# A median found from a bracket with two ends, folded coefficients, and another order of the input, at the head of a conv-attention-MoE layer

## The chip, the cores and the metric

The kernel runs on one core of a Trainium2 chip. The metric is the device time of one execution in microseconds (us); the median of three runs is given. Engines are named as in the profile: PE is TensorE's matmuls and PEld its weight loads, DVE is VectorE, ACT is ScalarE, POOL is GpSimd, SP is SyncE, which issues most DMAs.

## The reference

The input x is 8 batches of 512 channels of 16 x 16. The layer normalises x by groups of 16 channels, gates each channel by its own statistics, and goes on with windowed attention (16 heads) and a mixture of 8 experts over 2048 tokens. The change touches the gate alone:

```
xf = x.reshape(b, c, h * w)                       # x: normalised by groups
mean, mx, std = mean(xf), max(xf), std(xf, ddof=1)     # over 256 places, per channel
u = stack([mean, mx, std], axis=-1)               # per batch 512 * 3 = 1536 numbers
med = median(u.reshape(b, -1), axis=-1)           # mean of the 768th and the 769th
u = (u - med) ** 3
z = einsum('bck,ck->bc', u, cfc_w) / sqrt(1 + eps) * bn_w + bn_b
return x * sigmoid(z)                             # and x + this goes on as tokens
```

## The kernel before

All 8 batches of x lie in SBUF as T, channels on partitions (4 blocks of 128). SyncE loads them in the order 0 to 7 (L427), one semaphore each, then the attention's weights.

Statistics. For batches 0 to 3 ScalarE makes the sums and, after a pass with the means, the sums of squares (L699 to L709); VectorE makes the maxima of all 8 batches and the statistics of batches 4 to 7 (L967 to L973). A matmul with a group matrix gives the group's mean, another its variance. ScalarE then splits two pieces of the weights, loads the table for the square root, and takes it (L719). VectorE computes u, 128 partitions by 8 batches x 12 numbers (4 blocks, 3 kinds), and three copies spread so that TensorE's transposes put each batch's 1536 numbers on 16 partitions.

Median. In 8 rounds, each of the 16 partitions of a batch tests a threshold; VectorE and ScalarE count half of the numbers each, and a matmul adds the 16 answers, so the interval narrows by 16 in each round (L1041 to L1061). `low` is then a lower bound within the last width. What follows is exact: `low` is brought from the 128 threshold partitions to 96 rows (one for each batch, block and kind, holding 128 channels, `uT`); the numbers at most `low` are counted and the least above it is found; count and least go by transposes to one partition, where the 768th number is chosen; that goes back to the 96 rows, the same count and least are made for it, and the 769th is chosen; half their sum goes to all partitions by a matmul. These are five exchanges between VectorE and TensorE (`med_in`, `med_out`).

Coefficients. VectorE cubes u - med, multiplies by the weights, adds the three kinds, scales by the norm's constant and weight, adds its bias; ScalarE takes the exponential; VectorE forms the sigmoid, multiplies by 1/deviation and gets the two coefficients for each batch and channel (L1119 to L1142).

Then `affine(0)` applies them to batch 0 (L1145), TensorE transposes it to tokens (L1619), ScalarE copies the tokens, VectorE and GpSimd normalise them, TensorE transposes again and begins the projections. `keep_busy(n)` is n matmuls of the identity whose result nobody reads (L1570); each is two passes in the trace. They stand where TensorE would else be idle: 10, then 8 ahead of the rounds, 9 behind the median, 16 behind the first transposes. The order on each engine is as written; there is no scheduler. What stands behind (attention, experts, adding the experts' results into the output by a chain of DMAs) is the same in both versions.

Of the kernel before, what the change touches and what calls it, by code (L numbers as in the profile page):

```python
# [17 lines left out]
B, C, S = 8, 512, 256  # L18
# [3 lines left out]
P = 128  # L22
CB = C // P
# [3 lines left out]
UK = 3  # L27
ACT_STATS = 4
UP = CB * UK
MED_N = C * UK  # L30
CNT = 17
# [77 lines left out]
def layer_kernel(nc, x, params, wqkvo, gate, ws, wgu, wd, out):  # L109
    ctx = ExitStack()  # L110
    with ctx:

        def sb(name, shape, dt=fp32, scope=ctx):
            return scope.enter_context(nc.sbuf_tensor(name, shape, dt))
# [55 lines left out]
        row = sb("row", [1, 8, B * UP], fp32, scope)  # L170
        g_avg = sb("g_avg", [P, P], fp32, scope)
        spread = sb("spread", [P, B * UP], fp32, scope)
        col = sb("col", [B * UP, 24], fp32, scope)
        sb("below_rden", [P, 8], fp32, scope)
# [47 lines left out]
        u = vf[:, 0:B * UP]  # L222
        uw = vf[:, B * UP:4 * B * UP].rearrange("p (k n) -> p k n", k=3)
        uT = vf[0:B * UP, 4 * B * UP:4 * B * UP + P]
        junk = vf[0:B * UP, 4 * B * UP + P:4 * B * UP + 4 * P].rearrange("p (k n) -> p k n", k=3)

        is_below = vf[:, 4 * B * UP + 4 * P:4 * B * UP + 4 * P + 1].bitcast(bf16)[:, 0:1]
        block_sum = vf[:, 4 * B * UP + 4 * P + 2:4 * B * UP + 4 * P + 2 + P // 2].bitcast(bf16)
        iota_i = qf[:, 512:512 + P].bitcast(i32)
        token_i = qf[:, 768:768 + 2 * NT].bitcast(i32)  # L230
        every_u = [front[:, 0:512], front[:, 512:1024], x2[:, 0:512]]
# [104 lines left out]
        z_ready, ez_ready = sem("z_ready"), sem("ez_ready")  # L336
# [68 lines left out]
        NCONSTS = 7  # L405
# [106 lines left out]
        def _(pool):  # L512
            pool.wait_ge(fills_done, NFILLS)
            for t, base, pattern, mult, fill, op in (
# [3 lines left out]
                (spread[:, :].rearrange("p (a c) -> p a c", c=UP), 0, [[-THRESHOLDS, B], [0, UP]], 1, 1.0,  # L518
                 ALU.not_equal),
# [3 lines left out]
            pool.wait_ge(consts_done, 4)  # L523
# [166 lines left out]
        def _(act):  # L690
# [4 lines left out]
            cols = [(b, k, CB * b + k) for b in range(ACT_STATS) for k in range(CB)]  # L695
            na = CB * ACT_STATS
            unread = [t[:, S * k:S * (k + 1)] for t in (front, x2T, x2) for k in range(CB)]
            unread += [probs[:, k, 0:S] for k in range(CB)]
            for b, k, c in cols:  # L699
                act.wait_ge(x_loaded[b], 16)  # L700
                ins = act.activation(unread[c], at(T, b)[:, k * S:(k + 1) * S], ACT.Copy,
                                     accum_out=small[:, 12, c:c + 1])
            ins.then_inc(act_sums, 1)
            act.wait_ge(act_sums, 1)
            act.activation(small[:, 13, 0:na], small[:, 12, 0:na], ACT.Copy, scale=-1.0 / S).then_inc(act_sums, 1)
            act.wait_ge(act_sums, 2)
            for b, k, c in cols:
                ins = act.activation(unread[c], at(T, b)[:, k * S:(k + 1) * S], ACT.Square,
                                     bias=small[:, 13, c:c + 1], accum_out=small[:, 5, c:c + 1])  # L709
            ins.then_inc(act_sums, 1)  # L710
# [19 lines left out]
            act.activation(small[:, 15, :], small[:, 14, :], ACT.Exp, scale=-1.0).then_inc(ez_ready, 1)  # L730

# [205 lines left out]
        def _(dve):  # L937
# [8 lines left out]
            fill(spread[:, :], 0.0)  # L946
# [3 lines left out]
            lo, bound, cnt = col[:, 0:1], col[:, 1:2], col[:, CNT:CNT + 3]  # L950
# [13 lines left out]
            n.n = 4  # L964


            for b in range(B):  # L967
# [23 lines left out]
            dve.wait_ge(act_sums, 2)  # L991
# [6 lines left out]
            dve.wait_ge(act_sums, 3)  # L998
# [19 lines left out]
            dve.wait_ge(root_ready, 1)  # L1018
            dve.wait_ge(dve_step, step_of(dve.reciprocal(inv2, root)))
# [5 lines left out]
            u3 = u.rearrange("p (n k) -> p n k", k=UK)  # L1025
# [10 lines left out]
            dve.tensor_tensor(u3[:, :, 0], K(7), r, ALU.mult)  # L1036
            dve.tensor_tensor(u3[:, :, 1], K(10), r, ALU.mult)
            dve.scalar_tensor_tensor(u3[:, :, 2], root2[:, n32:2 * n32], 0.5, r, ALU.mult, ALU.mult).then_inc(u_ready, 1)
# [3 lines left out]
            for i, width in enumerate(WIDTHS):  # L1042
# [8 lines left out]
                if i == 0:  # L1051
                    dve.wait_ge(uT_full, 1)
                    dve.wait_ge(dve_step, step_of(dve.tensor_copy(uT, PS[6][0:B * UP, 0:P])))
# [6 lines left out]
                else:  # L1060
                    ins.then_inc(med_in, 1)  # L1061

            def least(dst, bound):

                dve.wait_ge(dve_step, step_of(dve.tensor_scalar(junk[:, 0, :], uT, bound, BIG, ALU.is_le, ALU.mult)))
                dve.wait_ge(dve_step, step_of(dve.tensor_tensor(junk[:, 1, :], junk[:, 0, :], uT, ALU.add)))
                return dve.tensor_reduce(dst, junk[:, 1, :], AX.X, ALU.min)

            def of_batch(k):
                return row[0:1, k, :].rearrange("p (b n) -> p b n", b=B)  # L1070


            def by_batch(t):
                return t.rearrange("p (b n) -> p b n", b=B)

            dve.wait_ge(med_out, 1)
            dve.wait_ge(dve_step, step_of(dve.tensor_copy(lo, PS[4][0:B * UP, 384:385])))
            step_of(dve.tensor_scalar(junk[:, 2, :], uT, lo, 0.0, ALU.is_le, ALU.add, accum_out=cnt[:, 1:2]))
            step_of(least(cnt[:, 0:1], lo))
# [932 lines left out]
```

## Time and profile before

| | |
|---|---|
| median of 3 runs | 718.38 us (717.37 to 720.6) |
| profiled execution | 718.36 us |
| its span, first to last instruction | 716.6 us |
| busy: PE, PEld, DVE, ACT, POOL | 649.3, 553.2, 443.4, 335.8, 317.5 us |
| mean granted TensorE clock | 0.965 |

The span is counted from the first instruction. A row of a timeline tells when an instruction or a group of like ones started, how long it was busy, and in brackets how long its engine idled before it and what ended that. Granted clock is the share of 2.4 GHz that TensorE was given: 1.00 or 0.50.

### The profile page before, as it was taken

The page shows a single profiled execution, that of the slowest core. Times are in us where ns is not written, and L with a number is a line of the kernel's source. Part 1 is how long each engine was busy: PE and PEld are TensorE (multiplying, and loading weights), DVE is VectorE, ACT ScalarE, POOL GpSimd, SP SyncE. Part 2 cuts the span into 40 slices and gives each one's busy share as a digit, 9 for nine tenths or more (in the row PEclk, how much of TensorE's full clock was granted, in tenths as well). Part 3 has the DMA queues.
Part 4 walks back from the last instruction along what each step waited for, and adds up shares of the span by engine and source line. Part 5 has one row for each costly group of instructions (what it writes and reads, how often), then busy time and mean ns, then how long its engine had stood idle before and what let it go on. Part 6 is the DMA issues. An engine that isn't in the chain of part 4 may idle for free.

```text
span 716.6 us, 14422 instructions
## 1 busy us (share of the span) xinstructions
PE 649.3 (91%) x5030; PEld 553.2 (77%) x5031; DVE 443.4 (62%) x974; ACT 335.8 (47%) x616; POOL 317.5 (44%) x377
## 2 busy tenths in 40 slices
PE   1417989999999999999999999999899999999991
PEld 1407878888888888887789899999677877778771
DVE  7875454757575757573646995223676767667761
ACT  7641364646464646465523123434444454444540
POOL 1340343646464646462421115856345455454534
PEclk9758999999999999999999999999999999999996
DMA  9800000101010101020226323452865555556543
GB/s 307 340 0 1 1 2 1 60 1 59 0 59 0 59 0 59 1 90 1 90 76 240 116 91 113 130 176 70 299 115 96 112 98 107 105 100 111 99 70 44
DMA packets 24787, 62.62 MB, mean 87 GB/s; under 512 B 3056, under 2 KB 7920, under 8 KB 23216
## 3 DMA queue, kind: packets, MB, share of 16 engines
q1 hardware_dynamic: 14912, 41.69, 16.3%
q0 software_dynamic: 9168, 20.45, 15.7%
q8 instruction: 21, 0.34, 0.2%
q10 hardware_dynamic: 672, 0.03, 0.1%
q14 instruction: 14, 0.11, 0.0%
HBM read 39.09 MB, written 23.07 MB: 87 GB/s over the span
## 4 chain that ended last, share of the span: by engine, by line
PE 53%; DMA 27%; DVE 10%; issue 4%; POOL 3%; ACT 1%; DVEq 1%; SPq 0%; POOLq 0%; ACTq 0%
DMA out_tokens<-yo,dest 24%; PE PS L1566 21%; PE scores L1566 12%; PE scores L1858 5%; PE PS L1686 4%; PE scores L1670 3%; PE PS L1635 2%; PE PS L1693 1%; DMA out_tokens<-T 1%; DVE rden L1203 1%; DMA T<-in_x 1%; DVE front L1046 1%; POOL out_tokens L668 1%; PE PS L1624 1%; DVE front L1150 1%
## 5 line engine op out<-in xcount | busy, mean ns | idle before, releaser
L1566 PE MATMUL scores<-xb,sw_h 128*128 128x256 f32 x512 | 94.6, 285 | 0.0
L659 POOL DMA_INDIRECT out_tokens<-yo,dest x36 | 57.1, 1586 | 79.6 <-DMA out_tokens<-yo,dest 77.3
L1566 PEld LDWEIGHTS scores<-xb,sw_h 128*128 128x128 f32 x512 | 81.2, 192 | 2.2 <-ACT probs L757 0.4
L1566 PE MATMUL PS<-xt_h,w_h 128*128 128x256 f32 x256 | 74.5, 291 | 1.6 <-DVE xt_l L1188 1.6
L1566 PE MATMUL scores<-xb,sw_l 128*128 128x256 f32 x256 | 72.5, 283 | 0.0
L1566 PE MATMUL PS<-xt_l,w_h 128*128 128x256 f32 x256 | 72.4, 283 | 0.0
L1566 PE MATMUL PS<-xt_h,w_l 128*128 128x256 f32 x256 | 72.3, 283 | 0.0
L558 POOL TENSOR_SCALAR_AFFINE_SELECT probs<-probs 128x256 f32<-128x256 f32 x128 | 50.4, 418 | 45.6 <-ACT probs L761 45.4
L1566 PE MATMUL scores<-wgu_h,xgT_h 128*128 x156 | 65.0, 417 | 2.1 <-DVE xgT_l L1528 2.1
L1203 DVE RECIPROCAL rden<-PS 128x256 f32<-128x256 f32 x32 | 56.1, 1753 | 13.5 <-PE PS L1686 11.8
L577 POOL TENSOR_TENSOR hl<-hf,hh 128x256 fp32r<-128x256 f32 x32 | 28.5, 890 | 76.3 <-ACT hh L839 76.3
L1566 PE MATMUL scores<-wgu_h,xgT_l 128*128 x156 | 61.1, 391 | 0.0
L907 ACT ACTIVATE wdt_h<-wd_sb 128x512 fp32r x76 | 43.9, 624 | 36.4 <-PE scores L1566 36.4
L1566 PE MATMUL scores<-wgu_l,xgT_h 128*128 x156 | 60.9, 390 | 0.0
L757 ACT ACTIVATE probs<-scores 128x768 f32<-128x768 f32 x64 | 51.3, 802 | 11.2 <-PE scores L1670 11.1
L761 ACT ACTIVATE probs<-probs 128x768 f32<-128x768 f32 x64 | 54.1, 846 | 2.0
L1523 DVE TENSOR_TENSOR wdt_l<-wd_sb,wdt_h 128x512 fp32r<-128x512 f32 x76 | 49.1, 688 | 9.3 <-ACT wdt_h L907 7.6
L1566 PEld LDWEIGHTS PS<-xt_h,w_h 128*128 128x128 f32 x256 | 49.0, 191 | 4.8 <-issue 3.0
L571 POOL TENSOR_TENSOR att_l<-att,att_h 128x256 fp32r<-128x256 f32 x32 | 23.8, 744 | 63.8 <-ACT att_h L765 63.7
L1566 PEld LDWEIGHTS scores<-xb,sw_l 128*128 128x128 f32 x256 | 49.1, 192 | 0.0
L1566 PEld LDWEIGHTS PS<-xt_l,w_h 128*128 128x128 f32 x256 | 49.0, 192 | 0.0
L1566 PEld LDWEIGHTS PS<-xt_h,w_l 128*128 128x128 f32 x256 | 49.0, 192 | 0.0
(304 smaller groups left out, 1623.6 us busy)
## 6 DMA issues: line engine op xcount, KB each, us to landing
wgu_l<-in_wgu SPq DMA_DIRECT2D x8, 1024.0 KB, 7.7
T<-in_x SPq DMA_DIRECT2D x8, 512.0 KB, 7.9
w_in<-in_wqkvo SPq DMA_DIRECT2D x4, 1024.0 KB, 12.1
x_rows<-x SPq DMA_DIRECT2D x8, 512.0 KB, 2.8
x_cols<-x2T SPq DMA_DIRECT2D x8, 512.0 KB, 2.6
xc<-x_cols SPq DMA_DIRECT2D x8, 512.0 KB, 3.9
out_tokens<-T SPq DMA_DIRECT2D x8, 512.0 KB, 7.8
wd_sb<-in_wd SPq DMA_DIRECT2D x8, 512.0 KB, 6.9
```

The costliest lines, as they stand in the source:

```text
L558: ins = pool.affine_select(out=t, in_=t, compare_op=ALU.is_ge, fill=0.0, base=0, pattern=[[0, 2], [1, P]], channel_multiplier=-1)
L571: pool.tensor_tensor(att_l[:, c, :], att[:, :], att_h[:, c, :].bitcast(fp32), ALU.subtract).then_inc(att_l_done, 1)
L577: pool.tensor_tensor(hl[:, j, :], hf[:, j % 2, :], hh[:, j, :].bitcast(fp32), ALU.subtract).then_inc(hl_done, 1)
L659: pool.indirect_dma_start(out[:, :], bass.IndirectOffsetOnAxis(dest[:, t:t + 1], 0), yo[:, t % 3, :], None, compute_op=ALU.add).then_inc(y ...
L757: act.activation(probs[:, p % 4, :].rearrange("p (h q) -> p h q", h=2), scores[:, 2 * (p % 2):2 * (p % 2) + 2, 0:384], ACT.Tanh, scale=1.0 ...
L761: act.activation(probs[:, p % 4, :], probs[:, p % 4, :], ACT.Exp, scale=SOFTCAP).then_inc(exp_done, 1)
L907: act.activation(wdt_h[:, k * C:(k + 1) * C], w[:, k * C:(k + 1) * C], ACT.Copy).then_inc(wdt_h_done, 1)
L1203: dve.wait_ge(dve_step, step_of(dve.reciprocal(rden[:, :], od_bank[:, S:2 * S])))
L1523: dve.tensor_tensor(wdt_l[:, k * C:(k + 1) * C], w[:, k * C:(k + 1) * C], wdt_h[:, k * C:(k + 1) * C].bitcast(fp32), ALU.subtract).then_in ...
L1566: ins = pe.matmul(out, lhs(k, a), rhs(k, b), start=m == 0, stop=m == len(products) - 1)
L1686: ins = pe.matmul(od_bank[j * D:(j + 1) * D, off + tt * P:off + S], lhs(h, tt), pr[:, 0:S] if tt == 0 else pr[:, S:S + P], start=tt == 0, ...
L1858: ins = pe.matmul(dn_bank[tt], (hh, hl)[a][:, j, tt * P:(tt + 1) * P], shared_slice(c, 2, j, 0, C), start=j == 0 and m == 0, stop=j == CB ...
```

## The change

1. SyncE loads x in the order 0, 1, 4, 2, 5, 3, 6, 7, and VectorE takes the batches in that order. ScalarE makes sums and squares for batches 0 and 1, and then for 2 and 3.
2. Each batch's 12 numbers lie in 16 places of u (the others hold a large number), so that the transpose has 128 rows, 16 for a batch, like the thresholds: `low` needs no exchange. An upper end `high` is `low` plus the last width and a rounding allowance. VectorE finds in each row the least number from `low` up, the negative of the greatest up to `high`, the least above `high`, and the count up to `high`. One matmul brings the four to 8 partitions, one for each batch; there the upper of the two middle numbers is the greatest up to `high`, or the least above it if the count falls short, and so on; a matmul of ones with a diagonal brings half the sum to all partitions.
3. The norm's constant and weight are multiplied into the convolution's weights beforehand (`weights3`); 1 + exp(-z) is multiplied by the deviation before the reciprocal.
4. Of `affine(0)`'s four blocks ScalarE makes two, with an Identity activation with scale and bias from the coefficients.
5. `keep_busy(9)` becomes `keep_busy(8)`.

```diff
-            for b in range(B):
+            for b in ARRIVAL:
                 sp.dma_start(at(T, b).rearrange("p (k s) -> p k s", k=CB),
...
+            for first, group in enumerate(((0, 1), (2, 3))):
+                these = [(b, k, CB * b + k) for b in group for k in range(CB)]
...
+            act.wait_ge(coef_ready, 1)
+            for k in (2, 3):
+                ins = act.activation(front[:, k * S:(k + 1) * S], at(T, 0)[:, k * S:(k + 1) * S], ACT.Identity,
+                                     bias=coefB[:, k:k + 1], scale=coefA[:, k:k + 1])
+            ins.then_inc(y0_upper, 1)
...
+            step_of(dve.tensor_scalar(deviation, root2[:, 0:n32], 0.5, None, ALU.mult))
+            dve.wait_ge(prm_loaded, 16)
+            step_of(dve.scalar_tensor_tensor(
+                weights3.rearrange("p (c k) -> p c k", k=UK), prm[:, 0:UP].rearrange("p (c k) -> p c k", k=UK), bn_scale,
+                prm[:, UP:UP + CB].unsqueeze(2).to_broadcast([P, CB, UK]), ALU.mult, ALU.mult))
...
+            size_step = step_of(dve.scalar_tensor_tensor(low_size, low, -1.0, low, ALU.mult, ALU.max))
+            from_low = step_of(dve.tensor_scalar(least_of[:, 0, :], uT, low, BIG, ALU.is_lt, ALU.mult))
+            dve.wait_ge(dve_step, size_step)
+            dve.wait_ge(dve_step, step_of(dve.tensor_scalar(low_size, low_size, 3.0 / 2 ** 23, WIDTHS[-1], ALU.mult,
+                                                            ALU.add)))
+            high_step = step_of(dve.tensor_tensor(high, low_size, low, ALU.add))
+            step_of(dve.tensor_tensor(least_of[:, 0, :], least_of[:, 0, :], uT, ALU.add))
+            dve.wait_ge(dve_step, high_step)
+            counted = step_of(dve.tensor_scalar(least_of[:, 2, :], uT, high, 0.0, ALU.is_le, ALU.add,
+                                                accum_out=cols[:, 3:4]))
+            over_high = step_of(dve.tensor_scalar(least_of[:, 1, :], uT, high, BIG, ALU.is_gt, ALU.mult))
+            dve.wait_ge(dve_step, counted)
+            step_of(dve.scalar_tensor_tensor(least_of[:, 2, :], least_of[:, 2, :], BIG, uT, ALU.mult, ALU.add))
+            dve.wait_ge(dve_step, over_high)
+            dve.wait_ge(dve_step, step_of(dve.tensor_tensor(least_of[:, 1, :], least_of[:, 1, :], uT, ALU.subtract)))
+            dve.wait_ge(dve_step, step_of(dve.tensor_reduce(cols[:, 0:3], least_of, AX.X, ALU.min)))
+            dve.tensor_tensor(cols_of, cols.unsqueeze(2).to_broadcast([P, 4, UM]),
+                              own_slot.unsqueeze(1).to_broadcast([P, 4, UM]), ALU.mult).then_inc(med_in, 1)
             dve.wait_ge(med_out, 1)
...
+            dve.wait_ge(dve_step, step_of(dve.tensor_reduce(count, by_slot[:, 3, :], AX.X, ALU.add)))
+            step_of(dve.tensor_reduce(rows[:, 0:3], by_slot[:, 0:3, :], AX.X, ALU.min))
...
+            dve.tensor_scalar(diagonal, ident[0:B, 0:B], both, 0.5, ALU.mult, ALU.mult).then_inc(med_in, 1)
...
+            dve.wait_ge(dve_step, step_of(dve.scalar_tensor_tensor(K(0), K(15), 1.0, deviation, ALU.add, ALU.mult)))
+            dve.wait_ge(dve_step, step_of(dve.reciprocal(K(2), K(0))))
...
+                for k in range(2 if isinstance(b, int) and b == 0 else CB):
...
+            pe.matmul(PS[4][0:B, 384:384 + 4 * UM], own_batch, cols_of.rearrange("p k j -> p (k j)"), start=True,
+                      stop=True).then_inc(med_out, 1)
             pe.wait_ge(med_in, 2)
+            pe.matmul(PS[6][:, 0:B], ones[0:B, :], diagonal, start=True, stop=True).then_inc(med_out, 1)
...
+                if part == "lead":
+                    pe.wait_ge(y0_upper, 1)
...
-            keep_busy(9)
+            keep_busy(8)
```

How the instructions stand on the engines is shown at three places. Names are those of the program: qT, kT, v and x (for x2) also hold the small tables of this stage, T is the input. First VectorE over the batches of the input, before:

```order
L973 TENSOR_REDUCE qT<-T 128x4 x4
L972 BN_STATS qT<-T 128x6 x4
L973 TENSOR_REDUCE qT<-T 128x4
L972 BN_STATS qT<-T 128x6 x4
L973 TENSOR_REDUCE qT<-T 128x4
L972 BN_STATS qT<-T 128x6 x4
L973 TENSOR_REDUCE qT<-T 128x4
L972 BN_STATS qT<-T 128x6 x4
L973 TENSOR_REDUCE qT<-T 128x4
```

and in the change:

```order
L987 TENSOR_REDUCE qT<-T 128x4 x2
L986 BN_STATS qT<-T 128x6 x4
L987 TENSOR_REDUCE qT<-T 128x4 x2
L986 BN_STATS qT<-T 128x6 x4
L987 TENSOR_REDUCE qT<-T 128x4 x2
L986 BN_STATS qT<-T 128x6 x4
L987 TENSOR_REDUCE qT<-T 128x4
L986 BN_STATS qT<-T 128x6 x4
L987 TENSOR_REDUCE qT<-T 128x4
```

A maximum (TENSOR_REDUCE) alone is a batch of ScalarE's; a maximum behind four BN_STATS is one of VectorE's own. Before, the four lone ones stood first; now the second and third stand between VectorE's own.

Then TensorE from the last round of the search (L1595, L1593) to the first transposes of batch 0 (L1624, L1615), before:

```order
L1595 MATMUL PS<-v 128x1 x8
L1598 MATMUL PS<-med,spread 96x1
L1600 MATMUL PS<-ident,col 1x96
L1601 MATMUL PS<-ident,col 1x96
L1602 MATMUL PS<-ident,col 1x96
L1604 MATMUL PS<-ones,row 96x1
L1606 MATMUL PS<-ident,col 1x96
L1607 MATMUL PS<-ident,col 1x96
L1609 MATMUL PS<-row,ones 128x8
L1574 MATMUL scores<-ident 128x128 x9
L1624 MATMUL PS<-ident,front 128x128 x8
```

and in the change:

```order
L1593 MATMUL PS<-v 128x1 x8
L1595 MATMUL PS<-x,qT 8x64
L1598 MATMUL PS<-x,ones 128x8
L1572 MATMUL scores<-ident 128x128 x8
L1615 MATMUL PS<-ident,front 128x128 x8
```

Of eight small instructions in five exchanges two are left, and the filler behind them has one matmul less.

Last VectorE from the last update of the bound (L1055, L1082) up to what TensorE carries to the place of the choice; before, with the first instruction behind that (L1083):

```order
L1055 SCALAR_TENSOR_TENSOR med<-PS,med 128x1
L1077 COPY col<-PS 96x1
L1078 TENSOR_SCALAR v,col<-v,col 96x128
L1065 TENSOR_SCALAR v<-v,col 96x128
L1066 TENSOR_TENSOR v<-v 96x128
L1067 TENSOR_REDUCE col<-v 96x1
L1083 TENSOR_REDUCE row<-PS 1x8
```

and in the change, up to the product that TensorE takes (L1106):

```order
L1082 SCALAR_TENSOR_TENSOR med<-PS,med 128x1
L1090 SCALAR_TENSOR_TENSOR x<-med 128x1
L1091 TENSOR_SCALAR v<-v,med 128x128
L1093 TENSOR_SCALAR x<-x 128x1
L1095 TENSOR_TENSOR x<-x,med 128x1
L1096 TENSOR_TENSOR v<-v 128x128
L1098 TENSOR_SCALAR v,x<-v,x 128x128
L1100 TENSOR_SCALAR v<-v,x 128x128
L1102 SCALAR_TENSOR_TENSOR v<-v 128x128
L1104 TENSOR_TENSOR v<-v 128x128
L1105 TENSOR_REDUCE x<-v 128x3
L1106 TENSOR_TENSOR x<-x,qT 128x64
```

Before, a copy of the bound from TensorE stands at the head, and the same four instructions come again later for the second number. Now eleven instructions stand in one piece, over 128 rows and for both ends, and the copy is gone.

## Rows read from the trace of the kernel before

**Rows 1.** Page, chain that ended last, shares of the span by engine.
```profile
PE 53%; DMA 27%; DVE 10%; issue 4%; POOL 3%; ACT 1%; DVEq 1%; SPq 0%; POOLq 0%; ACTq 0%
```

**Rows 2.** Windows: stretch, length; busy PE, PEld, DVE, ACT, POOL; clock; DMA, GB/s.
```profile
46.55:55.28 8.73, 2.70 (x12) 1.69 (x12) 4.96 (x27) 1.15 (x1) 0.00 (x0) 0.50 0.00 0
...
54.65:59.20 4.55, 4.55 (x20) 4.41 (x20) 3.21 (x14) 0.23 (x1) 0.00 (x0) 0.50 0.01 4
59.40:60.09 0.69, 0.00 (x0) 0.00 (x0) 0.64 (x2) 0.00 (x0) 0.00 (x0) 1.00 0.00 0
```

**Rows 3.** Timeline of VectorE, statistics: start, duration, engine, line, operation, tiles, [idle before].
```profile
8.13 1.22 DVE L973 TENSOR_REDUCE qT<-T 128x4 f32<-128x1024 f32 x1 [0.42 <-DMA T<-in_x]
...
11.29 1.41 DVE L972 BATCH_NORM_STATS2 qT<-T 128x6 f32<-128x256 f32 x4 [0.28 <-DMA T<-in_x]
12.62 1.20 DVE L973 TENSOR_REDUCE qT<-T 128x4 f32<-128x1024 f32 x1
...
21.15 0.19 DVE L988 TENSOR_TENSOR kT<-qT 128x16 f32<-128x16 f32 x1
21.25 0.18 DVE L989 TENSOR_TENSOR kT<-qT 128x16 f32<-128x16 f32 x1
```

**Rows 4.** Timeline of ScalarE: sums, squares, table load, square root.
```profile
11.00 0.40 ACT L701 ACTIVATE probs<-T 128x256 f32<-128x256 f32 x1
...
12.28 0.49 ACT L708 ACTIVATE front<-T,kT 128x256 f32<-128x256 f32 x1
...
21.67 1.28 ACT L719 ACT_TABLE_LOAD   x1
24.48 0.26 ACT L719 ACTIVATE kT<-kT 128x64 f32<-128x64 f32 x1 [1.52 <-DVE kT L1012]
```

**Rows 5.** Timeline of VectorE: last bound update, median, its subtraction.
```profile
46.55 0.16 DVE L1055 SCALAR_TENSOR_TENSOR med<-PS,med 128x1 f32<-128x1 f32 x1 [0.28 <-PE PS L1595]
...
47.48 0.34 DVE L1078 TENSOR_SCALAR_CACHE_REDUCE v<-v,col 96x128 f32<-96x128 f32 x1
...
47.75 0.28 DVE L1065 TENSOR_SCALAR v<-v,col 96x128 f32<-96x128 f32 x1
48.06 0.29 DVE L1066 TENSOR_TENSOR v<-v 96x128 f32<-96x128 f32 x1
48.38 0.28 DVE L1067 TENSOR_REDUCE col<-v 96x1 f32<-96x128 f32 x1
49.46 0.25 DVE L1083 TENSOR_REDUCE row<-PS 1x8 f32<-1x96 f32 x1 [0.79 <-PE PS L1602]
...
55.28 0.26 DVE L1119 TENSOR_TENSOR v<-v,PS 128x96 f32<-128x96 f32 x1 [0.68 <-PE PS L1609]
```

**Rows 6.** Timeline of VectorE: norm's scale, product with the deviation, affine step.
```profile
56.73 0.19 DVE L1130 SCALAR_TENSOR_TENSOR kT<-kT,prm 128x32 f32<-128x32 f32 x1
...
58.04 0.19 DVE L1139 TENSOR_TENSOR kT<-kT 128x32 f32<-128x32 f32 x1
...
58.66 1.38 DVE L1150 TENSOR_SCALAR front<-T,coefA,coefB 128x256 f32<-128x256 f32 x4
```

**Rows 7.** Timeline of TensorE: fillers and transposes.
```profile
14.42 4.37 PE L1574 MATMUL scores<-ident 128*128 128x128 f32 x20 [14.42 <-DMA T<-in_x]
...
55.17 4.21 PE L1574 MATMUL scores<-ident 128*128 128x128 f32 x18
60.09 1.09 PE L1624 MATMUL PS<-ident,front 128*128 128x128 f32 x8 [0.71 <-DVE front L1150]
61.02 3.74 PE L1574 MATMUL scores<-ident 128*128 128x128 f32 x32
65.80 1.09 PE L1635 MATMUL PS<-ident,front 128*128 128x128 f32 x8 [1.04 <-DVE front L1173]
```

**Rows 8.** Chain in order of time: start, duration, what.
```profile
68.51 11.74 PE PS L1566 x96
```

More of the change, by code:

```diff
@@ L693, in _ @@
             act.dma_start(gate_sb[:, :, 0:E], gate).then_inc(gate_loaded, 16)
[L695 to L696 removed]
             unread = [t[:, S * k:S * (k + 1)] for t in (front, x2T, x2) for k in range(CB)]
             unread += [probs[:, k, 0:S] for k in range(CB)]
[L699 to L710, printed above, removed]
+            for first, group in enumerate(((0, 1), (2, 3))):
+                these = [(b, k, CB * b + k) for b in group for k in range(CB)]
+                lo, hi = CB * group[0], CB * (group[-1] + 1)
+                for b, k, c in these:
+                    act.wait_ge(x_loaded[b], 16)
+                    ins = act.activation(unread[c], at(T, b)[:, k * S:(k + 1) * S], ACT.Copy,
+                                         accum_out=small[:, 12, c:c + 1])
+                ins.then_inc(act_sums, 1)
+                act.wait_ge(act_sums, 3 * first + 1)
+                act.activation(small[:, 13, lo:hi], small[:, 12, lo:hi], ACT.Copy, scale=-1.0 / S).then_inc(act_sums, 1)
+                act.wait_ge(act_sums, 3 * first + 2)
+                for b, k, c in these:
+                    ins = act.activation(unread[c], at(T, b)[:, k * S:(k + 1) * S], ACT.Square,
+                                         bias=small[:, 13, c:c + 1], accum_out=small[:, 5, c:c + 1])
+                ins.then_inc(act_sums, 1)
             def high_piece(m):
@@ L1060, in _ @@
                 else:
[L1061 to L1070, printed above, removed]
@@ new lines, in _ @@
+            at_low, minus_high, over, count, apart, second, both = [rows[:, k:k + 1] for k in range(7)]
+            dve.wait_ge(dve_step, step_of(dve.tensor_reduce(count, by_slot[:, 3, :], AX.X, ALU.add)))
+            step_of(dve.tensor_reduce(rows[:, 0:3], by_slot[:, 0:3, :], AX.X, ALU.min))
+            dve.wait_ge(dve_step, step_of(dve.tensor_scalar(apart, count, MED_N / 2 + 0.5, BIG, ALU.is_lt, ALU.mult)))
+            dve.wait_ge(dve_step, step_of(dve.scalar_tensor_tensor(second, at_low, apart, over, ALU.add, ALU.min)))
@@ L1088, in _ @@
+            dve.wait_ge(dve_step, step_of(dve.tensor_tensor(both, second, minus_high, ALU.subtract)))
+            dve.tensor_scalar(diagonal, ident[0:B, 0:B], both, 0.5, ALU.mult, ALU.mult).then_inc(med_in, 1)
+            dve.wait_ge(med_out, 2)
             dve.wait_ge(dve_step, step_of(dve.tensor_tensor(
-                row[0:1, 5, 0:B], row[0:1, 5, 0:B], by_batch(PS[4][0:1, 256:256 + B * UP])[:, :, 0], ALU.add)))
+                uw[:, 0, :].rearrange(by_b, b=B), u,
+                PS[6][:, 0:B].unsqueeze(2).to_broadcast([P, B, UP]), ALU.subtract)))
```

149 lines of the change are left out of this document (52 added, 97 removed).

## The prediction, made before the changed kernel was run

> **What bounds the kernel now.** I read the chain that ended last first: PE carries 53% of the span and DMA 27%, VectorE only 10% [rows 1]. So three quarters of the span lie behind the stage that the change touches, and the question is whether that stage is itself a chain on which everything behind waits. The windows say so. Between the last round of the search and the coefficients (46.55 to 55.28) TensorE is busy 2.70 of 8.73 us, VectorE 4.96, GpSimd 0, and the DMA queues move nothing [rows 2]. No engine is full: one small instruction waits for the next, across VectorE and TensorE. Up to the first projection at 68.51 it stays like that, and from there on the chain is PE matmul after PE matmul (the first piece is 96 of them, 11.74 us [rows 8]). No load of the start is still on its way at 46.55, and what comes later is triggered by progress. So each us taken out of the chain before 60 should come off the end, and I carry it one to one.
>
> **Order of x.** VectorE reduces batches 0 to 3 in 1.2 each and idles for the next arrival (0.42 before 8.13); batches 4 to 7 cost it statistics and maximum, and their four start only at 11.29, so it ends at 21.15 [rows 3]. That is 9.86 for four such batches, and 1.11 for a lone maximum (1.20 less the 0.09 by which an instruction without a wait starts before its predecessor's end: 21.15, 21.25 and 0.19 [rows 3]). In the new order batch 4 takes the third slot. From 8.13: 9.86 + 2 x 1.11 = 12.08, so the end is at 20.21: a gain of 0.94. Arrivals hold it: the slots land 1.57 apart (8.13 for the third [rows 3], 14.42 for the seventh, on which TensorE waits in both versions [rows 7]), and by the sum each batch is asked for after that. The cover to check is ScalarE. It now changes twice from sums to squares; such a change costs 12.28 - 11.00 - 0.49 - 0.40 = 0.39 [rows 4]. Its table load moves from 21.67 to 22.06 and ends 1.28 later at 23.34; the square root, waited for at 24.48 after 1.52 of idling [rows 4], would be asked for at 23.54. So 0.2 of cover is left: the gain lies between 0.55, if ScalarE is 0.4 worse than that, and 0.94, and I take 0.94. The two small reductions of the identity and one fill stand before the first arrival; the new deviation and weights stand where VectorE waits for TensorE's transposes; I cost these at nothing (0.4 if that wait were gone).
>
> **The median.** The stretch from the last update of the bound to the subtraction of the median is 46.55 to 55.28 [rows 5], with five exchanges with TensorE; the trees of instructions show two now. I lay the new one out by two rules read from rows: with a wait, the next starts 0.03 after the end (48.06 + 0.29, next at 48.38 [rows 5]); without one, 0.09 before it [rows 3]. Durations: column-sized 0.16, 128-wide select 0.28, add or subtract 0.29, count 0.34 of which the accumulator's read frees the engine after 0.27 (0.28 at 47.75 follows it) [rows 5]. The new reduction over 3 x 128 has no row; between 0.28 for 128 [rows 5] and 1.20 for 1024 [rows 3] the line gives 0.54 (ends 0.28 and 0.84, three times the small one). The 64-wide product lies between 0.19 for 16 [rows 3] and 0.29 for 128 [rows 5]: 0.23. Step by step: two column operations and the select to 47.00, two column operations to 47.26, add 47.26, count 47.46, select over the upper bound 47.73, the two combinations 47.92 and 48.12, reduction 48.44, product 49.01, ended 49.24. The first exchange: an exchange with 8 moving columns held VectorE 0.68 [rows 5]; a pass of 128 columns takes 4.21/18 = 0.234 [rows 7], so 56 more columns in two passes add 0.20: 0.88. At 50.12 two short reductions of 0.22 (0.25 is the nearest row, over 96 [rows 5]), one beside a 0.16, then three more of 0.16: ended 51.23. The second exchange 0.68: the subtraction starts at 51.91. Gain 55.28 - 51.91 = 3.37. With the ends of the unknown prices (reduction +0.30, first exchange between 0.68 and 1.1, short reductions 0.16 to 0.25) it is 2.8 to 3.7.
>
> At this place a rule of the Trainium skill speaks against me. In the trace the operation at 21.25 starts 0.10 after one that lasts 0.19, since it doesn't wait for it; the waiting one at 48.38 starts 0.32 after one of 0.29 [rows 3, 5]. The page "VectorE: DVE Perf Modes", section "The DRAIN you can't avoid", says that the next operation doesn't start until the pipe has emptied, so that leaving out the semaphore saves nothing. The trace doesn't agree with that for these pairs. By the row the sum stands; by the rule each of the eight pairs that the new order leaves without a wait (six in the bracket, one before the exchange back, one in the cube) costs 0.12 more, 0.96 in all.
>
> **Coefficients.** With folded weights the scaling by the norm (0.19 + 0.03) and the product with the deviation (0.19 + 0.03) [rows 6] leave the path, and one of the four 96-wide products runs beside another (0.29 becomes 0.17): gain 0.56. Bounds 0.44 to 0.60: the overlap is the only part without a row of its own.
>
> **First affine step in halves.** VectorE's four take 1.38 from 58.66, and the transposes start at 60.09 [rows 6, 7]: 1.43. Now ScalarE ends last. Its 128x256 costs 0.40 without a pointer operand and 0.49 with one [rows 4]; with scale and bias as pointers I estimate 0.58. Two, overlapping by 0.09, and 0.04 to TensorE: 1.11, a gain of 0.32 (0.68 if both cost 0.40; 0.17 if they don't overlap). No table load stands ahead of them in the order. TensorE's filler has 16 passes instead of 18: it begins 0.11 before the subtraction (55.17 against 55.28 [rows 5, 7]), so at 51.80, and ends at 55.54; the transposes are free at 55.82. Cover 0.3 where it was 0.71.
>
> **What the clock takes back.** Before, TensorE ran without a gap from 54.65 at a granted clock of 0.50 (1.2 GHz) up to 59.20, and stood at 1.00 (2.4 GHz) by 59.40 [rows 2], so all eight transposes at 60.09 ran at the high level [rows 7]. The new ones come 4.5 after the matmul that starts this stretch; the rise came 4.55 to 4.75 after it. So part of them may run at the low level: 0.234 instead of 3.74/32 = 0.117 [rows 7], at most 8 x 0.117 = 0.94, at least 0. I take 0.3, as the same lag would touch the first two or three.
>
> Sum: 0.94 + 3.37 + 0.56 + 0.32 - 0.30 = 4.9. The profiled execution took 718.36 (span 716.6 and 1.76 around it), the median of the runs is 718.38, so no correction: 718.4 - 4.9 = **713.5**. By the rule of the page it would be 714.4.
>
> **Rivals.**
> 1. The section costs the upper ends: reduction 0.30, exchange 0.22, the ACT halves 0.15, the root 0.39 late, the clock 0.94 instead of 0.3. For it: the 0.2 of cover on ScalarE. Against: each has a nearer row. Gain 3.2, 715.2.
> 2. VectorE doesn't overlap what has no wait: 714.4, as worked out. Against it: 21.15 and 21.25 [rows 3]. The page named above would have it so.
> 3. The clock rises late, so that the second filler of 32 passes also runs at the low level: 7.5 instead of 3.74. It waited 1.04 at its end [rows 7], so 2.7 is lost and the transposes lose 0.94: 5.2 - 3.6 = 1.6, 716.8. For it: a shorter filler with a gap behind it. Against: the gap is 0.3 where 0.7 did no harm.
> 4. Slower: the clock stays at 0.50 into the projections. The 96 matmuls of 11.74 [rows 8] would double: 1.6 - 11.7, 728.5. It turns slower once 13 of the 96 run low, since each costs 0.12. Against: in this trace the level rose after each such stretch of PE work, before any of them.
>
> **Chances.** Forecast 0.72, rivals 0.08, 0.08, 0.09 and 0.03. A measurement of this kernel can't tell less than 0.5% (3.6 us) from no change. Faster by more: the forecast but for 0.04, and most of rival 2: 0.74. Within: the rest of those, rival 3 and nearly all of rival 1: 0.22. Slower: rival 4 and 0.01 for what I don't see: 0.04. The range of the forecast alone is 712.3 to 714.7, with the unknown prices; reaching out to rival 1 and beyond it on both sides gives 711.9 to 716.0.
>
> **What would show it.** The maximum of the last batch ends 0.9 earlier; the square root starts with no idle time of ScalarE left or nearly; from the last bound update to the subtraction 5.4 instead of 8.73, with two waits for TensorE; the first transposes at 54.9 (55.82 less the 0.94); granted clock up before the second filler is half through; the same shift at 68.51 and at the first scatter-add. I am wrong if the round of the search changes, if the shift shrinks behind 68.51, or if the transposes wait for ScalarE more than 1.2 behind the coefficients.

## The result, and the profile after

| | before | after |
|---|---|---|
| median | 717.73 us (6 runs, 716.66 to 720.6) | 712.42 us (6 runs, 711.24 to 713.37) |
| profiled execution, its span | 718.36, 716.6 | 712.33, 710.5 |
| ratio | | 0.9917, 95% interval [0.9902, 0.9933] |

So the kernel is faster by 5.31 us in the medians, where 4.9 were forecast; 712.42 is 1.1 below the 713.5 of the forecast and inside its range. The chain of the changed kernel still lies on TensorE for half of the span (before: [rows 1]).

```profile
PE 51%; DMA 27%; DVE 10%; issue 7%; POOL 2%; ACT 1%; DVEq 1%; SPq 0%; POOLq 0%; ACTq 0%
```

The windows of the changed kernel cover the search's last update up to the subtraction of the median, from there to the first transposes, and the moment at which the clock rises (columns as in [rows 2]).

```profile
45.79:50.80 5.01, 1.01 (x5) 0.71 (x5) 3.58 (x20) 1.15 (x1) 0.00 (x0) 0.50 0.00 0
50.80:54.78 3.98, 3.67 (x16) 3.40 (x17) 2.94 (x12) 1.32 (x3) 0.00 (x0) 0.50 0.00 0
54.78:55.00 0.22, 0.22 (x1) 0.22 (x2) 0.00 (x0) 0.00 (x0) 0.00 (x0) 0.51 0.00 0
55.00:55.20 0.20, 0.20 (x3) 0.20 (x3) 0.00 (x0) 0.00 (x0) 0.00 (x0) 1.00 0.00 0
```

The stretch of 8.73 us is now 5.01. VectorE's share of it rose from 4.96 of 8.73 to 3.58 of 5.01: what went is mostly waiting. VectorE's timeline shows the statistics, the median and the coefficients (answering to [rows 3, 5, 6]).

```profile
8.04 1.41 DVE L986 BATCH_NORM_STATS2 qT<-T 128x6 f32<-128x256 f32 x4 [0.44 <-DMA T<-in_x]
...
20.16 0.19 DVE L1002 TENSOR_TENSOR kT<-qT 128x16 f32<-128x16 f32 x1
...
22.05 0.19 DVE L1019 COPY kT<-PS 128x32 f32<-128x32 f32 x1 [0.54 <-PE PS L1578]
...
45.79 0.16 DVE L1082 SCALAR_TENSOR_TENSOR med<-PS,med 128x1 f32<-128x1 f32 x1 [0.28 <-PE PS L1593]
45.98 0.16 DVE L1090 SCALAR_TENSOR_TENSOR x<-med 128x1 f32<-128x1 f32 x1
46.06 0.28 DVE L1091 TENSOR_SCALAR v<-v,med 128x128 f32<-128x128 f32 x1
...
47.18 0.28 DVE L1102 SCALAR_TENSOR_TENSOR v<-v 128x128 f32<-128x128 f32 x1
47.38 0.28 DVE L1104 TENSOR_TENSOR v<-v 128x128 f32<-128x128 f32 x1
47.70 0.55 DVE L1105 TENSOR_REDUCE x<-v 128x3 f32<-128x384 f32 x1
48.29 0.23 DVE L1106 TENSOR_TENSOR x<-x,qT 128x64 f32<-128x64 f32 x1
48.99 0.16 DVE L1113 TENSOR_REDUCE x<-PS 8x1 f32<-8x16 f32 x1 [0.47 <-PE PS L1595]
...
50.80 0.26 DVE L1122 TENSOR_TENSOR v<-v,PS 128x96 f32<-128x96 f32 x1 [0.68 <-PE PS L1598]
...
53.62 0.73 DVE L1148 TENSOR_SCALAR front<-T,coefA,coefB 128x256 f32<-128x256 f32 x2
```

Batch 4 is taken at 8.04, as soon as it has landed, and the statistics end at 20.16 instead of 21.15. Seven instructions of the bracket overlap the one ahead, in the way of the one at 46.06, which starts 0.08 before that of 45.98 has ended. The exchange that ends at 48.99 holds VectorE 0.47, less than any of the five before, which held it 0.56 to 0.79. TensorE's timeline has the exchanges, the fillers and the transposes ([rows 7]).

```profile
20.88 0.64 PE L1578 MATMUL PS<-kT,g_avg 128*128 128x32 f32 x2 [2.59 <-DVE kT L1007]
...
48.57 0.38 PE L1595 MATMUL PS<-x,qT 128*8 128x64 f32 x2 [2.82 <-DVE x L1106]
50.17 0.59 PE L1598 MATMUL PS<-x,ones 8*128 8x8 f32 x2 [1.22 <-DVE x L1118]
50.69 3.78 PE L1572 MATMUL scores<-ident 128*128 128x128 f32 x16
54.78 1.16 PE L1615 MATMUL PS<-ident,front 128*128 128x128 f32 x8 [0.31 <-ACT front L739]
55.78 3.74 PE L1572 MATMUL scores<-ident 128*128 128x128 f32 x32
60.54 1.09 PE L1626 MATMUL PS<-ident,front 128*128 128x128 f32 x8 [1.02 <-DVE front L1171]
63.25 0.36 PE L1564 MATMUL PS<-xt_h,w_h 128*128 128x256 f32 x1 [1.62 <-DVE xt_l L1186]
```

The first transposes take 1.16 where they took 1.09, the second filler 3.74 as before, and the projections start at 63.25 instead of 68.51. ScalarE's timeline has the square root and its half of the affine step ([rows 4]).

```profile
23.86 0.26 ACT L725 ACTIVATE kT<-kT 128x64 f32<-128x64 f32 x1 [0.68 <-DVE kT L1026]
...
53.54 1.09 ACT L739 ACTIVATE front<-T,coefB,coefA 128x256 f32<-128x256 f32 x2 [0.96 <-DVE coefB L1139]
```

The square root hangs on the group's mean. That came back later behind its matmul: 1.17 (20.88 on TensorE to 22.05 on VectorE), where before had 0.75:

```profile
21.87 0.64 PE L1580 MATMUL PS<-kT,g_avg 128*128 128x32 f32 x2 [3.09 <-DVE kT L993]
...
22.62 0.19 DVE L1005 COPY kT<-PS 128x32 f32<-128x32 f32 x1
```

By stages, worked out from the starts in the two timelines:

| stage, us | before | after | gain |
|---|---|---|---|
| start to arrival of the seventh batch | 14.42 | 14.33 | 0.09 |
| to the end of the statistics | 6.73 | 5.83 | 0.90 |
| to the count of the first round | 8.47 | 8.68 | -0.21 |
| the rounds | 16.93 | 16.95 | -0.02 |
| last update to subtraction of the median | 8.73 | 5.01 | 3.72 |
| to the affine step | 3.38 | 2.82 | 0.56 |
| to the first transposes | 1.43 | 1.16 | 0.27 |
| to the tokens' statistics | 1.92 | 1.97 | -0.05 |
| to the projections | 6.50 | 6.50 | 0 |
| sum | 68.51 | 63.25 | 5.26 |

The 5.26 arrive whole at the far end of the compute. There the experts' results are added into the output by DMAs, each waiting for the one ahead; the chains give the first and the last of them, before

```profile
517.37 4.86 DMA out_tokens<-yo,dest
...
702.16 3.79 DMA out_tokens<-yo,dest_halves
```

and after.

```profile
512.05 4.74 DMA out_tokens<-yo,dest
...
696.14 3.57 DMA out_tokens<-yo,dest_halves
```

The first starts 5.32 earlier, the last 6.02: 0.70 of the profiled pair's difference was won in that chain of DMAs (184.79 and 184.09), where nothing was changed. The experiments below ran on other chips, where before took 722.8 to 723.5, and there this chain lasted 186.4 to 191.0 in the profiled runs; both of these ends come from one chip. So I read effects below 2 us from stage times, and give ratios to the runs of before on the same chip. The change itself ran on the first chip and, once more, on that of the last experiment.

### The profile page after: what moved, and what is told of

It is laid out like the page before. It is cut to its first block, busy times and chain, and to the rows that moved or that the text cites. A ratio compares the mean times of both kernels' runs of the same rounds, so it can differ in the third digit from the quotient of the medians.

```text
span 710.5 us, 14396 instructions
## 1 busy us (share of the span) xinstructions
PE 644.2 (91%) x5021; PEld 549.5 (77%) x5022; DVE 441.5 (62%) x967; ACT 336.9 (47%) x619; POOL 316.9 (45%) x376
## 4 chain that ended last, share of the span: by engine, by line
PE 51%; DMA 27%; DVE 10%; issue 7%; POOL 2%; ACT 1%; DVEq 1%; SPq 0%; POOLq 0%; ACTq 0%
DMA out_tokens<-yo,dest 24%; PE PS L1564 20%; PE scores L1564 12%; PE scores L1849 5%; PE PS L1677 4%; PE scores L1661 3%; PE PS L1626 2%; PE PS L1684 1%; DMA out_tokens<-T 1%; DVE rden L1201 1%; DMA out_tokens<-yo,dest_halves 1%; DVE front L1073 1%; DVE qT L987 1%; DMA T<-in_x 1%; PE PS L1615 1%
```

## The experiments

The disputed sizes are four: the first exchange, the overlap of what does not wait, the clock, and what each part gives by itself. The main theory in the expectations is that of the prediction with its sizes corrected by the profile after.

**The old order of x.** The change with the batches in the order 0 to 7 and ScalarE's sums ahead of its squares.

```diff
-ARRIVAL = (0, 1, 4, 2, 5, 3, 6, 7)
+ARRIVAL = (0, 1, 2, 3, 4, 5, 6, 7)
...
-            for first, group in enumerate(((0, 1), (2, 3))):
+            for first, group in enumerate(((0, 1, 2, 3),)):
...
```

> The change with x loaded in the old order 0 to 7, and with ScalarE's sums of all four batches ahead of its squares; all else as in the change. Theory (VectorE's own batches set the end of the statistics): the last maximum ends at 21.1 instead of 20.16, and the first projection starts 0.9 later than 63.25, at 64.2; time 713.3. Rival (the root on ScalarE or the exchange for the group's mean takes most of that gain back, since the copy of the group's mean came only 0.57 earlier than before): the projection starts 0.3 to 0.6 later, at 63.7; time 712.9. The start of the copy of the group's mean behind its matmul tells: 0.75 behind the start of the matmul as before, or 1.17 as in the change.

Measured: ratio 0.9949 [0.9930, 0.9968]. From the seventh arrival (14.66) to the end of VectorE's statistics it is 6.75, as before the change:

```profile
20.17 1.20 DVE L987 TENSOR_REDUCE qT<-T 128x4 f32<-128x1024 f32 x1
21.41 0.19 DVE L1002 TENSOR_TENSOR kT<-qT 128x16 f32<-128x16 f32 x1
```

The order of x is worth 6.75 - 5.83 = 0.92 up to there (5.76 to 5.98 in the other runs with the new order); 0.94 was forecast. The first projection came at 65.22, 1.97 later than in the change and more than either theory had. Of the rest 0.33 is the arrival, 0.41 the stage to the first round and 0.31 the way from the subtraction on, where the transposes took 1.48; none of these is shown to hang on the order of x. The copy of the group's mean came 0.96 behind its matmul, neither 0.75 nor 1.17.

**No filler ahead of the first transposes.**

```diff
-            keep_busy(8)
             y_transposes("lead", 0, 0)
```

> The change without the 8 matmuls of the filler ahead of the first transposes. Theory (the filler is what raises the clock): granted clock 0.50 at the transposes, so the eight cost 0.9 more, and part of the second filler's 32 passes run at 0.234 instead of 0.117; the rise comes 4 to 5 us after the transposes begin, the second transposes start 1 to 2 us late; time 713.5 to 714.5. Rival (the clock follows the work behind as well, and the filler is idle ballast): the same time, 712.4. Rival 4 of the prediction (the clock stays low into the projections): 3.7 and more later, 716 to 728.

Measured: ratio 0.9939 [0.9916, 0.9963]. TensorE's timeline:

```profile
55.65 1.94 PE L1615 MATMUL PS<-ident,front 128*128 128x128 f32 x8 [4.01 <-ACT front L739]
57.38 5.06 PE L1572 MATMUL scores<-ident 128*128 128x128 f32 x32
62.28 1.04 PE L1626 MATMUL PS<-ident,front 128*128 128x128 f32 x8
```

After 4.01 of idling all eight transposes run at the low level (1.94 for 1.09), the clock rises only in the second filler (5.06 for 3.74), and VectorE's result no longer finds TensorE waiting. From the subtraction to the projections it is 13.27 instead of 12.45. But the 0.82 can't be put down to the filler. With the filler in place, the same eight transposes took 1.94 as well in two of the runs below, with a wait in every pair and with more filler:

```profile
55.49 1.94 PE L1620 MATMUL PS<-ident,front 128*128 128x128 f32 x8 [0.42 <-ACT front L739]
...
54.70 1.94 PE L1615 MATMUL PS<-ident,front 128*128 128x128 f32 x8 [0.31 <-ACT front L739]
```

There the same stretch is 13.30 and 13.19. Only the run without the filler shows so late a rise inside the second filler, and this cost 0.09 (6.59 instead of 6.50 from the tokens' statistics to the projections). What the filler is worth is therefore not shown. The run is rival 3 in kind, with at most 0.82 lost where the rival had 3.6.

**A wide weight in the first exchange.** The matmul that brings the four numbers to 8 partitions gets 128 weight columns (120 of them zero) instead of 8; beside that only a fill at the start is new, which makes the zeros.

```diff
...
-            pe.matmul(PS[4][0:B, 384:384 + 4 * UM], own_batch, cols_of
+            pe.matmul(PS[4][:, 384:384 + 4 * UM], own_wide, cols_of
...
```

> The change with the first exchange's matmul given 128 weight columns (8 real and 120 zero ones) instead of 8; 64 moving columns as before. It came back after 0.42 (matmul's start to VectorE's next), where I had put 0.88 for more moving columns. Theory A (the weight columns set such an exchange): it takes 0.75 to 0.85, the subtraction of the median starts 0.35 later. Theory B (the moving columns or the fixed part set it, and my price per column was wrong): it stays at 0.42.

Measured: ratio 0.9934 [0.9914, 0.9953]; last update to subtraction 5.32 instead of 5.01. The matmul on TensorE:

```profile
48.91 0.69 PE L1597 MATMUL PS<-x,qT 128*128 128x64 f32 x2 [2.81 <-DVE x L1108]
```

and VectorE's wait behind it:

```profile
49.63 0.16 DVE L1115 TENSOR_REDUCE x<-PS 8x1 f32<-8x16 f32 x1 [0.78 <-PE PS L1597]
```

0.69 instead of 0.38 and 0.78 instead of 0.47: the weight's width costs 0.31 here. (From the matmul's start to VectorE's next instruction it is 0.72 instead of 0.42, where theory A had 0.75 to 0.85.)

**A wait in every pair.** The nine instructions of the median and the cube that do not wait for their predecessor now do, on VectorE's own semaphore.

```diff
+            dve.wait_ge(dve_step, n.value())
             from_low = step_of(dve.tensor_scalar(least_of[:, 0, :], uT, low, BIG, ALU.is_lt, ALU.mult))
...
```

> The change with a wait for the instruction ahead put into all nine pairs of VectorE instructions between the last bound and the cube that had none. Theory (VectorE starts an instruction that waits for nothing 0.07 to 0.09 before the one ahead ends): each pair costs 0.10 to 0.12 more, 0.9 to 1.1 in all, from the last bound update to the cube's product. Rival (the next operation doesn't start until the pipe is empty, as the page on VectorE has it): no change, below 0.1.

Measured: ratio 0.9958 [0.9946, 0.9970]. The start of the bracket on VectorE:

```profile
45.39 0.16 DVE L1082 SCALAR_TENSOR_TENSOR med<-PS,med 128x1 f32<-128x1 f32 x1 [0.28 <-PE PS L1598]
45.59 0.16 DVE L1090 SCALAR_TENSOR_TENSOR x<-med 128x1 f32<-128x1 f32 x1
45.78 0.29 DVE L1092 TENSOR_SCALAR v<-v,med 128x128 f32<-128x128 f32 x1
```

The third starts 0.19 behind the second; in the change it was 0.08 (45.98 to 46.06). The median stretch is 6.00 instead of 5.01 and the coefficients 2.94 instead of 2.82: 1.11 in nine pairs, 0.12 each. The profile shows one thing more that no theory expected. Windows from the second filler into the projections, which start at 64.69 here:

```profile
59.00:64.30 5.30, 3.18 (x27) 2.75 (x25) 2.90 (x8) 1.09 (x2) 0.72 (x1) 1.00 0.00 0
64.40:67.60 3.20, 2.91 (x13) 2.94 (x14) 1.48 (x5) 0.00 (x0) 0.00 (x0) 0.50 0.00 0
67.80:71.00 3.20, 3.20 (x29) 3.20 (x28) 0.69 (x1) 0.00 (x0) 0.00 (x0) 1.00 0.00 0
```

After a stretch in which TensorE was busy 3.18 of 5.30, the granted clock was 0.50 in the first projections. The 13 matmuls of this window took 2.91, where 29 took 3.20 right behind: 2.91 - 13 x 0.11 is some 1.5 lost. This is rival 4 in small.

**The median alone undone.** The five exchanges of before with the other four parts of the change.

```diff
...
-            from_low = step_of(dve.tensor_scalar(least_of[:, 0, :], uT, low, BIG, ALU.is_lt, ALU.mult))
...
-            pe.matmul(PS[4][0:B, 384:384 + 4 * UM], own_batch, cols_of.rearrange("p k j -> p (k j)"), start=True,
-                      stop=True).then_inc(med_out, 1)
...
+            dve.wait_ge(dve_step, step_of(dve.tensor_copy(lo, PS[4][0:B * UP, 384:385])))
+            step_of(dve.tensor_scalar(junk[:, 2, :], uT, lo, 0.0, ALU.is_le, ALU.add, accum_out=cnt[:, 1:2]))
+            step_of(least(cnt[:, 0:1], lo))
...
+            step_of(least(cnt[:, 2:3], bound))
...
+            pe.matmul(PS[4][0:UPS, 384:385], spread[:, :], low, start=True, stop=True).then_inc(med_out, 1)
...
```

> The kernel before with the other four parts of the change (order of x, folded coefficients, affine step in halves, filler of 8), so the change without its new median. Theory (the five exchanges are the largest term, 3.7 of 5.3): from the last bound update to the subtraction 8.73 again instead of 5.01, the first projection 3.7 later than in the change, time between the two kernels: about 1.6 below before, ratio 0.998. Rival (the other parts carry more than I gave them, since the change's time fell by more than the forecast): ratio 0.996 or lower.

Measured: ratio 0.9974 [0.9961, 0.9987], and 8.72 from the last update to the subtraction (5.01 in the change). The median is worth 3.71 of the 5.26 up to the projections, the rest together 1.55.

**The affine step whole on VectorE.**

```diff
...
-                for k in range(2 if isinstance(b, int) and b == 0 else CB):
+                for k in range(CB):
...
```

> The change with all four blocks of the first affine step on VectorE, as before. Theory (ScalarE's half ends last at 1.16 behind the coefficients where VectorE alone needs 1.43): the transposes start 0.27 later behind the coefficients, and run at the high level; the first projection 0.1 to 0.3 later behind the subtraction of the median. Rival (the later transposes come behind the rise of the clock, which gives the 0.27 back): 0.0.

Measured: ratio 0.9954 [0.9933, 0.9975]; from the affine step to the transposes 1.43 instead of 1.16, so the halves are worth 0.27. The ratio is further from the change's than 0.27 would bring it, but the intervals touch, and the stages up to the projections show only 0.43 beside it, most of it in the stage to the first round (9.05) and in the transposes, which were expected at the high level and took 1.35. I can't tell that from the scatter of the runs.

**A longer filler at the head.** In the change the granted clock is 0.50 in part of the statistics; twice the filler at the arrival of the seventh batch was to keep it up.

```diff
-            keep_busy(10)
+            keep_busy(20)
```

> The change with 20 instead of 10 matmuls of the filler at the head, so that TensorE has work up to the group's mean. Theory (the clock's level between the group's mean and the spread transposes is a matter of when TensorE last had work, and costs 0.7): granted clock 1.00 from the group's mean to the end of the spread transposes; from the end of the statistics to the first round 8.0 instead of 8.68; ratio to before lower by 0.001. Rival (the return of the group's mean is longer at the high level: it took 0.96 in two runs with 1.00 and 0.74 in two with 0.50, so nothing is won): 8.5 to 8.7, no difference.

Measured: ratio 0.9924 [0.9902, 0.9945], not to be told from the change. The head was faster: 7.92 instead of 8.68 from the end of the statistics to the first round, though that stage took anything from 7.96 to 9.30 in the variants with ten fillers there, and 8.45 in the second profile of the change, so what the longer filler gives there is not told by one run. But the clock fell in the projections (first at 63.41), as the windows show:

```profile
56.00:62.70 6.70, 4.82 (x42) 4.39 (x40) 3.38 (x9) 1.70 (x4) 0.72 (x1) 1.00 0.00 0
62.90:69.50 6.60, 6.09 (x28) 6.12 (x29) 2.29 (x6) 0.00 (x0) 0.00 (x0) 0.50 0.00 0
69.70:75.00 5.30, 5.30 (x47) 5.30 (x46) 0.69 (x1) 0.00 (x0) 0.00 (x0) 1.00 0.01 3
```

28 matmuls in 6.09 busy us, where 47 took 5.30: 6.09 - 28 x 0.113 is 2.9 lost. Runs of this kernel spread from 715.45 to 722.4 and only one of them was profiled, so whether it falls in each is not shown.

**Seven rounds.** One round less (the bracket is 16 times wider, so the median is exact where no third number lies in it).

```diff
-ROUNDS = 8
+ROUNDS = 7
...
```

> The change with 7 rounds of the search instead of 8; the bracket's last width is 16 times as wide (4.8e-7), and the median is exact only if no third number lies in it. The piece of the weights that ScalarE splits in the eighth round comes behind the seventh. Theory (the rounds are a chain of 2.165 each and nothing else waits there): first projection 2.2 earlier, ratio to before 0.9887. Rival (GpSimd's eight low pieces of the weights, 14.2 from the first round on, or ScalarE's last piece and table load end later than the rounds, and hold the projections or the exponential): 0 to 1 earlier, ratio 0.9905 or more.

Measured: ratio 0.9904 [0.9881, 0.9927]; the rounds 14.79 instead of 16.95, the projections at 61.13 instead of 63.25. One round is 2.16, all of it on the path up to the projections. At the end of the kernel it isn't shown: the interval holds the 0.9887 of the theory and the 0.9905 of the rival.

**Fillers where the clock fell, the same with seven rounds, and the change again.** The three shared a chip and the runs of before.

```diff
-            keep_busy(10)
+            keep_busy(20)
...
-            keep_busy(16)
+            keep_busy(18)
             front_transposes("front", 0, 0)
+            keep_busy(5)
```

> The change with more filler on TensorE: 20 instead of 10 filler transposes at the head, 18 instead of 16 ahead of the second transposes, and 5 more behind them, ahead of the projections. Theory (the clock at the head is a cost of its own, and the change left TensorE with less to do before the projections): the granted clock stays at 1.00 from its rise in the second filler on through the 96 projection matmuls, with no fall at 62 to 70 us as in the run with the longer filler at the head alone; from the end of the statistics to the end of the first round 7.95 us (8.68 in the change); behind the projections nothing differs; ratio to the kernel before about 0.991, against 0.992 to 0.993 for the change itself on the same chip. Rival: the fillers stand in TensorE's queue ahead of work that is ready, so that the projections start 0.3 to 0.6 us later than they would and what the clock gives is given back: ratio 0.993 or more.

> The same fillers with seven rounds of the search instead of eight (the bracket is eight times wider; the median is exact as long as no third number lies in it). Theory: one round is 2.16 us, all of it on the path, so the projections start 2.16 us earlier than with the fillers alone and the ratio to the kernel before is about 0.003 lower, near 0.988. Rival: the shorter search leaves TensorE's filler at another point of the clock's course, the transposes or the projections run at the low clock, and less than 1 us of the 2.16 is left at the end: ratio 0.990 or more.

> The change itself once more, with nothing altered, to have it on the chip and beside the runs of the two others. Every theory expects the ratio of the first timing, 0.990 to 0.993; if it comes out above 0.994, part of the difference between the change and its variants of the earlier runs belongs to the chip and not to the variants.

| | median | ratio to before | first projection |
|---|---|---|---|
| the change again | 718.7 (5 runs) | 0.9933 [0.9920, 0.9947] | 63.43 |
| more filler | 717.49 (6 runs) | 0.9919 [0.9905, 0.9932] | 63.91 |
| more filler, seven rounds | 713.42 (4 runs) | 0.9855 [0.9840, 0.9870] | 59.71 |

The change comes out at 0.9933, a little above the 0.990 to 0.993 expected and below the 0.994 that would have laid part of the variants' differences on the chip; its interval overlaps that of the first timing. The fillers alone brought the head to 7.92, where 7.95 was expected (8.45 in the change beside them), and kept the clock at 1.00 into the projections (64 to 70). But their first projection came 0.48 later than in the change beside them: the seventh batch arrived 0.21 later, and 0.84 was lost from the subtraction on, with the first transposes at 1.94. And their profiled run lost the clock once further on:

```profile
64.00:70.00 6.00, 6.00 (x51) 6.00 (x52) 1.85 (x6) 0.00 (x0) 0.00 (x0) 1.00 0.01 3
80.00:87.40 7.40, 5.47 (x47) 4.27 (x49) 4.22 (x4) 5.19 (x8) 7.31 (x11) 1.00 0.00 0
87.60:90.80 3.20, 3.20 (x34) 2.51 (x27) 1.19 (x1) 0.84 (x1) 0.97 (x3) 0.50 0.02 5
```

This is a place that no filler here reaches, behind a stretch with 5.47 of 7.40 busy. The intervals of the two kernels overlap: what the fillers alone give is not shown. With seven rounds (the expectation's bracket eight times wider is a slip for sixteen) the interval lies below all others, 0.0078 under the change, where the expectation had some 0.005; the round's 2.16 is 0.0030 of that, so some 3 us are left to explain. On TensorE of that kernel

```profile
51.34 1.06 PE L1617 MATMUL PS<-ident,front 128*128 128x128 f32 x8 [0.31 <-ACT front L741]
...
59.71 0.36 PE L1566 MATMUL PS<-xt_h,w_h 128*128 128x256 f32 x1 [0.50 <-issue]
```

the transposes run at the high level. But so they did in the change beside it (1.06), and from the subtraction to the projections both took 12.35, so the fillers won nothing there. The first projection is 3.72 earlier than in that change: 2.16 is the round, 0.69 an earlier arrival of the seventh batch, 0.21 the statistics and 0.67 the stage to the first round, where the longer filler stands ahead. Behind the projections the two profiled runs show no gain: they took 714.34 and 715.8, 1.46 apart, as the chain of scatter-adds lasted 190.1 and 186.4. This is the fastest kernel of the study by its median; that its further gain is the clock's is not shown; the stages bear out 0.67 of it at most.

## Why the mechanism held, and where the sizes failed

The mechanism held: the head is a chain of small waits, and what is taken out of it arrives one to one at the first scatter-add (5.26 at the projections, 5.32 there). The step that failed is a size, the price of the first exchange in the median's term. The terms, in the order of the sum:

- **Order of x**, 0.94: 0.90 in the profiled pair, 0.92 by undoing it. But the cover on ScalarE was not what was late next: the square root, for which I expected no idle time or nearly none, still idled 0.68, since the group's mean came back from TensorE 0.42 later. The prediction has no term for that. At the first round 0.21 of it is left in this pair, and nothing in the second profile of the change, where the copy also took 1.17 but the whole stage 8.45 (8.47 before). I had not foreseen it, and can't explain it: the same instructions took 0.65 to 1.17 in the runs of the study.
- **Median**, 3.37: 3.72. What failed is "56 more columns in two passes add 0.20: 0.88" for the first exchange; it held VectorE 0.47. I took all of the 0.68 over from an exchange whose weight had 128 columns, and priced only what moves. With 128 weight columns it is 0.78 (the third experiment), so the weight's 8 columns save 0.31. What is left, 0.78 - 0.68 = 0.10 and not 0.20, is the 56 more moving columns together with whatever else differs between those two exchanges (the rows of the weight, the instruction that reads the result), which no run parts. Together that is the 0.41. (The Trainium skill's page "TensorE: Matmul & The Clock Gate", section "LDWEIGHTS (loading the stationary operand)", has the load's time go by the weight's columns, not its partitions; the third experiment agrees as to the columns, with 0.31 for 120 of them in two passes, and did not vary the partitions.) All else in the layout came out: the reduction 0.55 (0.54), the product 0.23 (0.23), the second exchange 0.68 (0.68), the product's start at 48.29, 2.50 behind the last update (2.46).
- **No overlap (rival 2)**: refuted. Adding the waits cost 0.12 a pair, the price that I had put on it, and there are nine pairs, not eight. The Trainium skill's page "VectorE: DVE Perf Modes", section "The DRAIN you can't avoid", has the next operation wait for the emptied pipe whether a semaphore stands between or not, and adds that one that is not held starts earlier. Of the two the rows bear out the second: 0.08 from start to start at 45.98 and 46.06 with no wait, 0.19 at 45.59 and 45.78 with one.
- **Coefficients**, 0.56: 0.56. **Halves**, 0.32: 0.27; ScalarE's two with pointers took 1.09 (1.07 estimated), but TensorE began 0.15 behind them (53.54 + 1.09, 54.78) where I had put 0.04.
- **Clock**, -0.30: -0.05 to -0.07 in this profile. It rose at 55.00, so that of the transposes only what ran in the first 0.22 was at the low level; I had put two or three there. That it came so early is in part luck. I had carried over the lag of one trace, and it is not fixed: behind the same filler the eight took 1.06 in the second profile of the change, and 1.06 to 1.94 in the variants, so the term could have been anything from 0 to -0.85. Rival 3 did not come: the second filler took 3.74. Nor did rival 4 in the change; it came in small in two of its variants.
- **Rival 1** needed all upper ends, and none came in the change; that of the clock nearly came in two variants (0.85 of 0.94).

The errors of the terms run against each other (median +0.35, clock +0.25, group mean -0.21, halves -0.05), and so 4.9 came close to 5.3, in part by luck. The error of 1.1 in the time is 0.4 from this and 0.7 from a reference: the forecast stood on 718.4, and six runs of before have a median of 717.73.

## What to carry to other kernels

Price a small exchange with TensorE by both operands: choose the orientation in which the weight has few columns. In a chain of small dependent instructions, interleave two chains so that no instruction waits for the one just ahead. Don't price a filler from one trace: behind the same filler the clock rose at different places here. And read a gain at the point where everything joins (here the first scatter-add), since what lies behind has its own scatter of several us.

## What the runs showed of the hardware that was not expected

- A weight of 8 columns against 128: the exchange 0.47 against 0.78, both with 64 moving columns in fp32 at a granted clock of 0.50.
- Behind the same exchange and the same filler, the eight first transposes took 1.06 to 1.94 us: from all at the high level to all at the low one.
- The granted clock was 0.50 in the first projections in two of the variants, over 13 and 28 matmuls of the windows shown. In both the stages ahead differed by under 1.2 us from those of the change, in which it did not fall there, and the first transposes had taken 1.94 and 1.86. In a third with 1.94, and with more filler behind, it did not fall there. What sets the place is open.
- The same chain of scatter-adds took 184.1 to 184.8 us on the first chip and 186.4 to 191.0 on the others, both ends of that on one chip: more than most edits here are worth.
